# Global attention: results divided by ScalarE and GpSimd, maxima split as columns and transposed through the score banks

## What is computed

```python
B, S, D = (2, 256, 128)
H = 16
DH = D // H
...
q = Q.reshape(b, s, H, DH).transpose(0, 2, 1, 3)
k = K.reshape(b, s, H, DH).transpose(0, 2, 1, 3)
v = V.reshape(b, s, H, DH).transpose(0, 2, 1, 3)
scores = jnp.einsum('bhqd,bhkd->bhqk', q, k) / jnp.sqrt(jnp.float32(DH))
attn = jax.nn.softmax(scores, axis=-1)
out = jnp.einsum('bhqk,bhkd->bhqd', attn, v)
```

## Time and profile before

| | us |
|---|---|
| median of 3 runs | 3771.01 |
| lowest, highest | 3766.46, 3773.81 |
| the profiled execution | 3774.6 |
| its span, first to last instruction | 3772.8 |
| PE, DVE busy in the span | 3613.5, 3193.1 |
| ACT, POOL busy in the span | 2811.2, 2403.1 |
| mean granted clock of TensorE | 0.984 |

### The profile page before, as it was taken

One profiled execution on the slowest core, in us unless ns is written; L12 is line 12 of the kernel. 1 busy time (PEld: TensorE's weight loads), 2 busy tenths in 40 slices (PEclk: granted clock), 3 DMA queues, 4 the chain that ended last, 5 costly groups with the idle time before them and its releaser, 6 DMA issues.

```text
span 3772.8 us, 160639 instructions
## 1 busy us (share of the span) xinstructions
PE 3613.5 (96%) x70220; PEld 2629.1 (70%) x70220; DVE 3193.1 (85%) x4678; ACT 2811.2 (75%) x4978; POOL 2403.1 (64%) x1986
## 2 busy tenths in 40 slices
PE   7999999959999999999999999999999999999997
PEld 2222222247888888888888888888888888888885
DVE  7999999668888888888888888888888888888884
ACT  3888888847777777777777777777777777777773
POOL 3100000067787778878787787778777787778883
PEclk7999999979999999999999999999999999999998
DMA  4110000024434444444444444444444444444442
GB/s 119 38 41 19 23 21 20 2 76 129 114 107 111 118 128 108 110 117 117 123 107 115 119 111 115 120 118 111 111 114 124 116 111 109 133 122 108 112 108 60
DMA packets 210249, 366.46 MB, mean 97 GB/s; under 512 B 37107, under 2 KB 81735, under 8 KB 209223
## 3 DMA queue, kind: packets, MB, share of 16 engines
q1 hardware_dynamic: 209482, 355.05, 35.4%
HBM read 236.73 MB, written 111.67 MB: 92 GB/s over the span
## 4 chain that ended last, share of the span: by engine, by line
PE 66%; DVE 6%; issue 2%; ACT 2%; POOL 2%; DMA 0%; DVEq 0%; POOLq 0%; SPq 0%; ACTq 0%
PE PA L1302 14%; PE PB L1378 10%; PE PD L1391 9%; PE PD L1330 7%; PE PB L1302 5%; PE PC L1352 5%; PE PC L1416 3%; PE PC L1425 3%; PE PA L1361 3%; DVE T L1655 3%; PE PC L1409 3%; DVE T L1660 3%; ACT SQ L1497 1%; PE PD L1294 1%; PE PC L1346 1%
## 5 line engine op out<-in xcount | busy, mean ns | idle before, releaser
L1212 POOL TENSOR_TENSOR T<-T 128x1024 f32<-128x1024 f32 x384 | 908.8, 2379 | 26.3 <-DVE T L1660 26.3
L1230 POOL TENSOR_TENSOR T<-T,rn 128x1024 f32<-128x1024 f32 x384 | 731.7, 1906 | 27.1 <-POOL rn L1223 0.4
L1302 PE MATMUL PA<-Wqkv,XS 128*128 128x512 f32 x2304 | 635.5, 411 | 10.8 <-DVE XS L1621 7.9
L787 ACT ACTIVATE E<-p_low 128x512 f32<-128x512 f32 x1024 | 556.1, 597 | 115.4 <-PE p_low L637 101.2
L716 DVE TENSOR_REDUCE negmax<-p_max 128x1 f32<-128x1024 f32 x512 | 589.1, 1217 | 20.1 <-PE p_max L616 20.1
L1302 PEld LDWEIGHTS PA<-Wqkv,XS 128*128 128x128 f32 x2304 | 418.5, 195 | 82.3 <-DVE XS L1621 10.7
L1668 DVE TENSOR_REDUCE ss<-SQ 128x32 f32<-128x2048 f32 x192 | 437.0, 2276 | 0.0
L1378 PEld LDWEIGHTS PB<-ET,VW 64*64 64x64 f32 x24576 | 377.6, 135 | 56.7 <-DVE T L1660 29.5
L1378 PE MATMUL PB<-ET,VW 64*64 64x32 f32 x24576 | 399.7, 220 | 18.0 <-DVE T L1660 8.7
L1330 PE MATMUL PD<-ident,T 128*128 128x128 f32 x3072 | 409.4, 276 | 6.2 <-POOL T L1230 5.0
L1391 PEld LDWEIGHTS PD<-Wo,OT 128*128 128x128 f32 x3072 | 367.5, 193 | 61.9 <-issue 61.7
(11 more groups left out here) (158 smaller groups left out, 6560.7 us busy)
## 6 DMA issues: line engine op xcount, KB each, us to landing
VW<-v_rows SPq DMA_DIRECT2D x768, 256.0 KB, 4.5
v_rows<-Vs SPq DMA_DIRECT2D x192, 512.0 KB, 6.0
Wraw<-in_Wqkv SPq DMA_DIRECT2D x40, 192.0 KB, 5.8
QA<-parts_q SPq DMA_DIRECT2D x384, 16.0 KB
KA<-parts_k SPq DMA_DIRECT2D x192, 32.0 KB
fs<-XC SPq DMA_DIRECT2D x48, 127.0 KB
parts_q<-AO SPq DMA_DIRECT2D x8, 384.0 KB, 2.6
parts_k<-AO SPq DMA_DIRECT2D x8, 384.0 KB, 3.3
```

What stands on the lines that cost most here:

```text
L787: act.activation(E[:, s % 4, c, :], p_s[:, (64 * g + i) % NS, :], ACT.Exp, scale=DH ** -0.5)\
L1212: pool.tensor_tensor(out=t_, in0=t_, in1=T2[:, i * HALF:(i + 1) * HALF], op=ALU.add).then_inc(ad.sem, 1)
L1230: pool.tensor_tensor(out=t_, in0=t_, in1=rn[:, p, i * LH:(i + 1) * LH].unsqueeze(2).broadcast_to([P, LH, LD]), op=ALU.mult).then_inc(no.se ...
L1302: mm = pe.matmul(pair[:, half, :], XS[:, b, i, 1:P + 1], Wqkv[:, l % 2, j, lo:lo + 512], start=(k == 0), stop=(k == 2))
```

## The change

**VectorE** no longer handles results. At the rows it works before the transposes instead of behind them: it splits the 16 columns of `negmax` into a bf16 part and a bf16 rest, `nmc` (128x16 each). **TensorE** transposes these two with a bf16 identity into one bank of the score ring, and the results too go through a bank of the ring instead of `p_max`. **ScalarE** copies the two sets of rows (16x256, bf16) to `nmb` in one instruction, and the transposed result back to `OE`. **GpSimd** then makes the reciprocal as a power of -1 and multiplies into `AO`. The ring has its own numbering, `ring`, over scores, rows and results. The rows come in the middle of steps 4 and 12, with no unit shifted; group 0 begins with 8 units of its second half, not 6, ahead of the first step. ScalarE's next copy into `OE` waits for GpSimd (`s_ao`), the row DMAs wait for ScalarE.

```diff
...
     def units(g, s):
 
-        if s < 5:
-            return [(g, 1, 6 + 2 * s + i) for i in range(2)]
+        if s < 4:
+            return [(g, 1, 8 + 2 * s + i) for i in range(2)]
...
     def begun_with(g):
 
-        return [(0, 0, i) for i in range(HU)], [(0, 1, i) for i in range(6)]
+        return [(0, 0, i) for i in range(HU)], [(0, 1, i) for i in range(8)]
...
+    def ring():
...
+        add("rows", 0, 0)
+        for g in range(NG):
+            for s in range(16):
+                add("score", g, s, 0)
+                add("score", g, s, 1)
+                if s == 4:
                     add("rows", g, 1)
-                if s == 13 and g + 1 < NG:
+                if s == 12 and g + 1 < NG:
                     add("rows", g + 1, 0)
...
+                add("score", g, s, 2)
+                add("score", g, s, 3)
                 if s == 3 and g > 0:
                     add("result", g - 1, 1)
                 if s == 11:
...
     def on_sp(sp):
...
         def max_rows(g, qh):
-            sp.wait_ge(s_mr.sem, s_mr.at(TURN["rows", g, qh]))
+            sp.wait_ge(s_ex.sem, s_ex.at(RING["rows", g, qh]))
...
     def on_pool(pool):
+
+        def result(g, qh):
+            b, hg = divmod(g, HG)
+            o = OE[:, qh, :].rearrange("p (q c w) -> p q c w", q=4, w=VW)
+            pool.wait_ge(s_ex.sem, s_ex.at(RING["result", g, qh]))
+            pool.tensor_tensor(out=rsum[:, qh, :, :], in0=o[:, :, :, DH], in1=minus[:, :, :], op=ALU.pow)\
+                .then_inc(s_rc.sem, 1)
+            pool.wait_ge(s_rc.sem, s_rc.at(g, qh + 1))
...
+            pool.tensor_tensor(out=a[:, :, hg, :, :], in0=o[:, :, :, 0:DH],
+                               in1=rsum[:, qh, :, :].unsqueeze(3).broadcast_to([P, 4, GH, DH]),
+                               op=ALU.mult).then_inc(s_ao.sem, 1)
...
             pool.tensor_copy(VG[:, g % 2, :, :, 0:DH + 1], VA[:, g // HG, :, heads(g), :]).then_inc(s_vg.sem, 1)
+            if g >= 2:
+                result(g - 2, 1)
+            if g >= 1:
+                result(g - 1, 0)
...
     def on_pe(pe):
...
         def max_rows(g, qh):
-            k = TURN["rows", g, qh]
-            pe.wait_ge(s_mr.sem, s_mr.at(k - 1))
-            pe.transpose(p_max[0:GH * 4, k % 2, 0:P], negmax[:, qh, :, :].rearrange("p c q -> p (c q)"),
-                         ident[:, :]).then_inc(s_mx.sem, 1)
+            n = RING["rows", g, qh]
+            pe.wait_ge(s_mb.sem, s_mb.at(g, qh + 1))
+            if n >= NS:
+                pe.wait_ge(s_ex.sem, s_ex.at(n - NS))
+            for j in range(2):
+                mm = pe.transpose(p_s[0:GH * 4, n % NS, :].bitcast(BF16)[:, j * P:(j + 1) * P], nmc[:, qh, j, :],
+                                  w["ident_b"][:, :])
+            mm.then_inc(s_st.sem, 1)
...
         def result(g, qh):
-            k = TURN["result", g, qh]
+            n = RING["result", g, qh]
             pe.wait_ge(s_oe.sem, s_oe.at(g, qh + 1))
-            pe.wait_ge(s_mr.sem, s_mr.at(k - 2))
+            pe.wait_ge(s_ex.sem, s_ex.at(n - NS))
             for qt in range(4):
-                mm = pe.transpose(p_max[:, k % 2, qt * P:(qt + 1) * P], OE[:, qh, qt * P:(qt + 1) * P], ident[:, :])
-            mm.then_inc(s_mx.sem, 1)
+                mm = pe.transpose(p_s[:, n % NS, qt * P:(qt + 1) * P], OE[:, qh, qt * P:(qt + 1) * P], ident[:, :])
+            mm.then_inc(s_st.sem, 1)
...
     def on_dve(dve):
...
         def max_rows(g, qh):
-            k = TURN["rows", g, qh]
-            dve.wait_ge(s_mx.sem, s_mx.at(k))
+            dve.wait_ge(s_mr.sem, s_mr.at(TURN["unit", g, qh, HU - 1]))
             if g > 0:
-                dve.wait_ge(s_md.sem, s_md.at(g - 1, 64 * (qh + 1)))
-            rows = p_max[0:GH * 4, k % 2, 0:P]
-            dve.tensor_copy(nmb[:, qh, 0, :], rows).then_inc(s_mb.sem, 1)
-            dve.wait_ge(s_mb.sem, s_mb.at(g, qh + 1))
-            dve.tensor_tensor(out=nmb[:, qh, 1, :], in0=rows, in1=nmb[:, qh, 0, :],
-                              op=ALU.subtract).then_inc(s_mr.sem, 1)
-
-        def result(g, qh):
...
-            dve.reciprocal(rsum[:, qh, :, :], o[:, :, :, DH]).then_inc(s_rc.sem, 1)
...
+                dve.wait_ge(s_st.sem, s_st.at(RING["rows", g - 1, qh]))
+            columns = negmax[:, qh, :, :].rearrange("p c q -> p (c q)")
+            dve.tensor_copy(nmc[:, qh, 0, :], columns).then_inc(s_nc.sem, 1)
+            dve.wait_ge(s_nc.sem, s_nc.at(g, qh + 1))
+            dve.tensor_tensor(out=nmc[:, qh, 1, :], in0=columns, in1=nmc[:, qh, 0, :],
+                              op=ALU.subtract).then_inc(s_mb.sem, 1)
...
     def on_act(act):
...
             if g > 0:
-                act.wait_ge(s_mx.sem, s_mx.at(TURN["result", g - 1, qh]))
+                act.wait_ge(s_ao.sem, s_ao.at(g - 1, qh + 1))
...
+        def max_rows(g, qh):
+            n = RING["rows", g, qh]
+            act.wait_ge(s_st.sem, s_st.at(n))
+            if g > 0:
+                act.wait_ge(s_md.sem, s_md.at(g - 1, 64 * (qh + 1)))
+            act.activation(nmb[:, qh, :, :].rearrange("r j n -> r (j n)"),
+                           p_s[0:GH * 4, n % NS, :].bitcast(BF16)[:, 0:2 * P], ACT.Copy).then_inc(s_ex.sem, 1)
+
+        def result(g, qh):
+            n = RING["result", g, qh]
+            act.wait_ge(s_st.sem, s_st.at(n))
+            act.activation(OE[:, qh, :], p_s[:, n % NS, :], ACT.Copy).then_inc(s_ex.sem, 1)
...
```

More of the change, by code:

```diff
@@ L465, in global_attention @@
     rsum = m.sb("rsum", [P, 2, 4, GH])
+    minus = m.sb("minus", [P, 4, GH])
     p_max = w["p_max"]
@@ L517, in turns @@
             add("unit", *u)
-        add("rows", 0, 0)
         for u in after:
@@ L540, in turns @@
         return at
-    TURN = turns()
+    RING = ring()
     def on_sp(sp):
@@ L601, in on_pool @@
                     .then_inc(w["l_w0s"].sem, 1)
+        result(NG - 2, 1)
+        result(NG - 1, 0)
+        result(NG - 1, 1)
         pool.wait_ge(s_gb.sem, NT + 1)
@@ L754, in on_dve @@
                 todo = units(g, s)
-                late = s % 8 == 5
-                if todo and not late:
-                    max_unit(*todo[0])
-                if s == 5:
+                if s == 4:
                     max_rows(g, 1)
-                if s == 13 and g + 1 < NG:
+                if s == 12 and g + 1 < NG:
                     max_rows(g + 1, 0)
-                if todo:
-                    max_unit(*todo[0 if late else 1])
-                if todo and late:
-                    max_unit(*todo[1])
-                if s == 3 and g > 0:
-                    result(g - 1, 1)
-                if s == 11:
-                    result(g, 0)
-        result(NG - 1, 1)
+                for u in todo:
+                    max_unit(*u)
     def on_act(act):
@@ L792, in on_act @@
                         result_copy(g, 0)
+                if s == 3 and g > 0:
+                    result(g - 1, 1)
+                if s == 11:
+                    result(g, 0)
                 if s == 13 and 2 <= g < 5:
```

88 lines of the change are left out of this document (43 added, 45 removed).

## The result

| | before | after |
|---|---|---|
| first comparison, median | 3768.74 us (4 runs) | 3738.52 us (4 runs) |
| second comparison of the same two kernels, median | 3768.43 us (17 runs) | 3729.59 us (6 runs) |
| the profiled execution | 3774.6 | 3726.18 |
| its span | 3772.8 | 3724.4 |

The ratio of the first comparison is 0.9909 (95% interval 0.9897 to 0.992), that of the second 0.9903 (0.9888 to 0.9918). So the kernel is faster by 0.9 to 1.0%, about 30 to 39 us; 3733 was forecast.

The account below looks back on a forecast made before the run. VectorE was taken to set the 20.68 us period, TensorE and ScalarE following closely. Terms -44.4 + 2 + 2.7 + 2 = -37.7 on the 3771.0 median gave 3733 us, range 3718 to 3757 leaving out B and C.

Parts of the forecast that it names:

- 30 periods: Global attention's repeating half-groups of 8 steps: each falls from 20.68 to 19.2 us, -44.4 in all, bounds -24 and -57.
- start: Before the first score: eight maximum units instead of six, 2.35 us more on VectorE, taken as +2 us.
- Wqkv conversions: Three conversions on ScalarE, 1.057 us each, lay in its slack and now lie on the full engine: +2.7 us.
- end: After the last result: copy back, power and multiply take 2.1 to 4.9 us against 0.9; +2 taken, +4 the bound.
- The working by events: One period summed from plain half-steps 13.26, first weighing's step 2.69, result's transposes to step 5 3.2: 19.15 us.
- The split of 0.5: At the rows, VectorE's added 128x16 cast and subtraction with handovers cost 0.5 us per period, bounds 0.4 to 0.7.
- -2.46: VectorE's loss per period: reciprocal, multiply and both 16x128 operations with their waits go, 2.46 us.
- VectorE's detour costs TensorE nothing there: At the rows, one unit later: the split falls under the 0.59 us of the result's transposes, so TensorE does not wait.
- ScalarE becomes the engine with the most work: Per period ScalarE needs 18.14 + 0.48 + 0.28 = 18.9 us, above VectorE's 18.7 and TensorE's 18.4.
- A: At the rows' transposes TensorE waits for VectorE's split, keeping half the gain: period 20.0, total 3757 us; chance 0.16.
- B: In the three-bank score ring, ScalarE idles 1.8 us or more per period: 3778 or 3806 us; chance 0.10.
- C: GpSimd's power keeps VectorE's subtraction from starting: 22.3 us needed per period, total 3826 us; chance 0.03.

Follow-up runs that it names:

- The two halves alone: Against the kernel before, only the results moved: period 20.35 us, ratio 0.9989; only the maxima's rows moved: period 19.16 us, ratio 0.9896.
- the first half: Only the results moved (score bank, ScalarE copy back, GpSimd division), rows as in the kernel before: period 20.35 us, median 3763.49 us, ratio 0.9989.
- its own experiment: Changed kernel plus a useless 128x16 GpSimd power beside VectorE's cast and subtraction: period 19.14 us, median 3738.50 us.

## Why the prediction was right, and where not

**The sum.** 3733 was forecast; the two medians, 3738.5 and 3729.6, lie on either side of it. On the stage alone the sum was -37.7 and the profiles show -37.9 and -37.1. Its terms:

| term | forecast | measured |
|---|---|---|
| 30 periods | -44.4 (20.68 to 19.2) | -46.0 (to 19.15) |
| start | +2 | +2.9 (first exponential 87.84 to 90.77) |
| Wqkv conversions | +2.7 | +1.8 |
| end | +2 | +3.5 |
| sum | -37.7 | -37.8 |

Their errors cancel, which is luck, so the sum is better than its parts. The working by events gave 19.15 and the engines' own needs 18.7, 18.9 and 18.4: it was the walk through one event, bank by bank, and not the ledger of any engine, that hit the period, down to the 0.3 of ScalarE's idle time and the score that waits for a bank (from the result's transposes to the next step it forecast 3.2 us; 409.52 to 412.74 are 3.22).

**Wqkv.** A period with such a conversion, by the copies back to `OE` (197.80, 217.55, 236.70):

```profile
197.80 0.60 ACT L807 ACTIVATE OE<-p_low 128x512 f32<-128x512 f32 x1 [0.29 <-PE p_low L710]
...
217.55 0.60 ACT L807 ACTIVATE OE<-p_low 128x512 f32<-128x512 f32 x1 [0.29 <-PE p_low L710]
...
236.70 0.60 ACT L807 ACTIVATE OE<-p_low 128x512 f32<-128x512 f32 x1 [0.29 <-PE p_low L710]
```

19.75 with it and 19.15 without, so 0.6 each instead of the 0.9 taken: the idle time that ScalarE still had may have taken the rest, of the 1.06 that a conversion lasts.

**The end.** ScalarE and GpSimd after the last weighing:

```profile
707.68 0.60 ACT L794 ACTIVATE OE<-p_low 128x512 f32<-128x512 f32 x1 [1.19 <-PE p_low L700]
```

```profile
709.70 2.90 POOL L604 TENSOR_TENSOR rsum<-OE,minus 128x16 f32<-128x16 f32 x1 [8.27 <-ACT OE L807]
...
713.40 0.10 POOL L883 MEMSET power<- 128x4 f32 x1 [0.32 <-POOLq L843]
```

From the last copy to the next part there are 5.72 us, where it was 2.22 (749.06 to 751.28). The power was mis-sized: 1.2 was taken and 3.6 set as the bound, 2.90 it is. The surplus goes nearly by columns after all, and the step that failed is the choice of the nearest row for a width four times as large.

**VectorE's ledger.** The split of 0.5 (0.37 to the next reduction in the timeline) was right in size. What was wrong is that "-2.46" was treated as one thing that the removed operations cost. The two halves alone show 0.33 and 1.52, and the results' share becomes 0.01 once the rows are moved. Nor did VectorE set the pace of the whole period before, as the prediction said: of the 1.53 us that the change won, 0.34 are TensorE's wait for the result's buffer, 1.04 the rows and the half-step behind them (1.75 + 1.92 became 1.52 + 1.11), and only 0.17 the stretch behind that, in which half-steps of 1.13, VectorE's pace, became 1.11. The kernel before with a lighter VectorE was not run. The prediction gave no price for the halves; had it given one, it would have been 0.8 for the results, as the expectation of the first half did.

**The mechanism at the rows.** "VectorE's detour costs TensorE nothing there" holds in the trace, and the cover is worth the 0.27 to 0.30 by which the split is late without it. But in the change as it stands it brings nothing: in steps 5 and 13 the split costs 0.30 and the ring 0.26 less. Only with the results inside step 4 does the place pay.

**Which engine.** "ScalarE becomes the engine with the most work", 18.9 us of work, was wrong, and so was the "floor" of 18.8 to 18.9 made of it. The 0.552 per exponential is TensorE's half-step halved; ScalarE alone needs 0.49. With 32 of those, 0.48 and 0.49 for the two copies of a result (the second 410.22 to 410.71) and 0.27 for the rows (411.66 to 411.93) its need is 16.9, an estimate from these rows. That is why lightening it by 0.8 brings 0.08, and only where exponentials stand in line behind the copies. TensorE's half-step of 1.107 paces all plain half-steps now; before the change five in a period went at VectorE's 1.13.

**The rivals.** A: TensorE did not wait at the rows; refuted by the trace (0.45 behind the weighing), and seen where the rows lie in step 5, 0.30. B: ScalarE's two waits are 0.29 and 0.19, far from 1.8. C: refuted for the power by its own experiment. But the prediction took a power for GpSimd's only work that could meet the split, and didn't price the bias additions. They do hold the split up where they meet it (3.2 us once, in the kernel with the rows only), and that they miss it in the change is luck.

## What to carry to other kernels

Where several engines run at nearly the same pace, an engine's ledger only gives a floor, and only if its price for one instruction is read where nothing holds the engine up (0.49 and not 0.552 for an exponential here); walk once through the place where the order breaks, buffer by buffer, and multiply by how often it comes. Price the parts of a change one by one in each other's presence: here one half carried all of the gain, and the other moved work off an engine that then waited. When the engines are level, the next gain is in the latency between them: give ScalarE two scores to work on while TensorE transposes (0.27 us per period), and measure two such shifts together, since here the second took the first one's 0.27 back.

## What was not expected of the hardware

A GpSimd power of 128x16 f32 took 2.90 us, one of 128x4 1.01 to 1.39 in the same profile, while a multiply of 128x128 took 0.41. A VectorE multiply out of PSUM and the cast behind it, which does not depend on it, start 0.20 apart (413.29 and 413.49), less than the 0.29 that the first is shown with. A cast and a subtraction with two SBUF inputs ran beside a power that had begun before them, at 0.17 and 0.18; beside additions of 128x512 the same two took 1.03 and 1.19 and ended as an addition ended. And the layers, the same instructions each time, took from 2823.6 to 2837.4 us in fourteen profiles, at a mean granted clock of 0.982 to 0.987.
